# Splitting each head's intra-tile product of a Mamba-2 mixer into two matmuls of 64 result rows

## The reference, cut to what matters

```python
def step(state, inp):
    dA_t, dt_t, B_t, C_t, x_t = inp
    dB = dt_t[:, :, None] * B_t[:, None, :]
    state = dA_t[:, :, None, None] * state + x_t[..., None] * dB[:, :, None, :]
    y = jnp.einsum('bn,bhpn->bhp', C_t, state)
    return (state, y)
...
_, ys = lax.scan(step, state0, xs)
y = ys.transpose(1, 0, 2, 3) + xh * D[None, None, :, None]
y = y.reshape(batch, seqlen, D_SSM)
yg = y * _silu(z)
yn = yg * lax.rsqrt(jnp.mean(yg * yg, axis=-1, keepdims=True) + EPS) * norm_w
return jnp.einsum('bld,ed->ble', yn, W_out)
```

## Time and profile before

| | |
|---|---|
| median of 3 runs | 1515.18 us |
| span of the profiled execution | 1514.6 us |
| PE busy | 1454.3 us (96%) |
| weight loads busy | 1258.6 us (83%) |
| DVE, ACT, POOL busy | 1049.3, 784.3, 788.9 us |
| mean granted TensorE clock | 0.981 |
| line L2184 on PE | 512 passes, 62.6 us busy |

### The profile page before, as it was taken

How to read it: one execution, slowest core, us unless ns; L and a number is a source line. 1 busy time by engine, 2 the same in 40 slices (tenths; PEclk the granted TensorE clock), 3 DMA queues, 4 the chain that set the end, 5 groups by cost and what they waited for, 6 DMA issues and landing times. The chain is left out here.

```text
span 1514.6 us, 22382 instructions
## 1 busy us (share of the span) xinstructions
PE 1454.3 (96%) x8274; PEld 1258.6 (83%) x8274; DVE 1049.3 (69%) x1750; ACT 784.3 (52%) x1343; POOL 788.9 (52%) x480
## 2 busy tenths in 40 slices
PE   6999999999999999999999999999999999999997
PEld 5878999989987687788788779779779999999875
DVE  6584666567556898789769869867746566676455
ACT  3312666666532467566656656645025666666311
POOL 3203777777535445645643753652026777776343
PEclk9899999999999999999999999999999999999998
DMA  8232787787544220020011011016226788876254
GB/s 311 84 115 86 262 279 263 259 278 269 207 155 125 79 88 1 29 70 29 9 62 56 1 43 56 20 32 231 67 82 217 260 280 287 275 259 243 91 161 145
DMA packets 79739, 222.15 MB, mean 147 GB/s; under 512 B 8400, under 2 KB 16592, under 8 KB 78224
## 3 DMA queue, kind: packets, MB, share of 16 engines
q1 hardware_dynamic: 57552, 163.04, 30.9%
q0 software_dynamic: 11360, 37.23, 8.3%
q10 hardware_dynamic: 10720, 20.45, 3.8%
HBM read 183.47 MB, written 37.22 MB: 146 GB/s over the span
## 5 line engine op out<-in xcount | busy, mean ns | idle before, releaser
L661 POOL TENSOR_TENSOR g_lo<-g_raw,g_hi 128x1408 fp32r<-128x1408 f32 x54 | 180.6, 3344 | 113.8 <-ACT g_hi L826 111.3
L661 POOL TENSOR_TENSOR u_lo<-u_raw,u_hi 128x1408 fp32r<-128x1408 f32 x54 | 174.6, 3233 | 59.2 <-ACT u_hi L826 59.1
L1861 PE MATMUL bank<-u_hi,xgT 128*128 128x352 f32 x624 | 168.5, 333 | 0.0
L1884 PE MATMUL bank<-d_hi,hT 128*128 128x512 f32 (+1 forms) x468 | 159.4, 395 | 5.4 <-DVE hT L1166 5.4
L1861 PE MATMUL bank<-g_hi,xgT 128*128 128x352 f32 x624 | 162.9, 323 | 0.0
L691 POOL DMA_INDIRECT xg<-token_x,row_of x78 | 87.9, 1127 | 138.7 <-DVE row_of L1311 122.4
L876 ACT ACTIVATE gate<-bank 128x512 f32<-128x512 f32 (+1 forms) x48 | 28.7, 598 | 213.4 <-PE bank L1814 212.5
L1829 PE MATMUL bank<-d_hi,hT 128*128 128x512 f32 (+1 forms) x384 | 130.7, 413 | 7.8 <-DVE hT L1166 7.6
L747 POOL TENSOR_TENSOR w_hl<-w_raw,w_hl 128x1024 fp32r<-128x1024 f32 x35 | 88.3, 2524 | 95.3 <-ACT w_hl L826 95.3
L721 POOL DMA_INDIRECT yg<-routed_y,slots x64 | 68.7, 1074 | 111.5 <-DVE X L1353 70.9
L1166 DVE TENSOR_TENSOR d_lo<-d_raw,d_hi 96x512 fp32r<-96x512 f32 (+2 forms) x54 | 121.4, 2249 | 0.0
(11 more groups left out here) (264 smaller groups left out, 3669.2 us busy)
## 6 DMA issues: line engine op xcount, KB each, us to landing
g_raw<-in_w_gate SPq DMA_DIRECT2D x54, 704.0 KB, 5.6
u_raw<-in_w_up SPq DMA_DIRECT2D x54, 704.0 KB, 6.9
d_raw<-in_w_down SPq DMA_DIRECT2D x46, 512.0 KB, 5.2
w_raw<-in_w_in SPq DMA_DIRECT2D x36, 512.0 KB, 3.5
routed_y<-ys ACTq DMA_DIRECT2D x32, 512.0 KB
d_raw<-in_w_down SPq DMA_DIRECT2D x46, 192.0 KB, 6.3
token_x<-xn SPq DMA_DIRECT2D x8, 1024.0 KB, 5.8
X<-in_x SPq DMA_DIRECT2D x4, 1024.0 KB, 10.4
```

The source lines that it names most:

```text
L661: pool.tensor_tensor(half_of(piece, 1, s), raw_at[piece][s % RING][:], half_of(piece, 0, s).bitcast(F), ALU.subtract)\
L1861: ins = pe.matmul(dst[:, 0:FE], xgT[:, n % 2, hx, kc], half_of(piece, hw, NS + j)[:, kc], start=(m == 0), stop=(m == 3 * KD - 1))
L1884: ins = pe.matmul(bank[Y + n % 2][:], hT[0:fw, hh, c, 0:P], half_of(2, hw, NS + j)[0:fw, c], start=(m == 0), stop=(m == 3 * NF - 1))
```

## The change

Each head's matmul becomes two. The first takes the first 64 columns of `L[:, h]` as stationary operand and writes rows 0 to 63 of the result, the second takes the last 64 columns and writes rows 64 to 127. The moving operand is the same 128x64 for both. Row and column of the place in the array follow from the operands: the built program holds these matmuls as tiles of 128 rows by 64 columns of the array, at column 0 and at column 64, in turn. Waits and signals stay where they were: a wait before the first matmul of a group, a signal with the last one of two groups.

```diff
                                 for h in range(g * GH, (g + 1) * GH):
-                                    ins = pe.matmul(bank[6 + h // 8][:, (h % 8) * HD:(h % 8 + 1) * HD], L[:, h],
-                                                    xdt[:, h * HD:(h + 1) * HD], start=True, stop=True)
+                                    for r in range(0, P, P // 2):
+                                        ins = pe.matmul(bank[6 + h // 8][r:r + P // 2, (h % 8) * HD:(h % 8 + 1) * HD],
+                                                        L[:, h, r:r + P // 2], xdt[:, h * HD:(h + 1) * HD],
+                                                        start=True, stop=True)
                                 if g % 2:
                                     ins.then_inc(m_E, 1)
```

## The result

The changed kernel takes 1503.43 us (median of 6 runs, 1502.57 to 1512.47), the kernel before 1516.52 us beside it (6 runs, 1514.74 to 1518.38). The ratio is 0.9919, 95% interval 0.9898 to 0.994. I had said 1507 us.

What follows compares the result with a forecast made beforehand. PE was taken to set the pace, in the mixer tile only just, with the burst paced by weight loads. Gains of 1.9 + 5.1 + 1.1 = 8.1 us gave 1507 us; range 1503 to 1545, the forecast's own 1503 to 1512.

Steps and rivals of the forecast that it cites:

- The burst goes at the pace of its loads, and the halves overlap: PE's burst in each mixer tile: both halves load and stream at once, 1.89 us instead of 3.58, 1.69 less.
- rival of one path: All weight loads share one path: +0 to +0.2 us a burst, about 1516 us, no change; chance 0.26.
- slower rivals: Each switch of half costs time (1561 us), or loads and streams don't overlap (1571 us); together chance 0.27.
- Entering and leaving the column tiles: Changing stationary shape around each of 16 bursts: 0 for 32 entries and exits; other end 0.09 each, 2.9 us.
- Tiles 1 and 2: Eight of 16 mixer tiles: POOL's chain limits the gain to 0.24 us each, 1.9 us in all.
- Tile 3: Last tile of a block, projections after it: all 1.69 us kept in three tiles, 5.1 us; the fourth counted 0.
- Tile 0: First tile of a block: 0 in two first blocks, 0.55 us each in two second blocks, 1.1 us.
- The sum: Whole mixer: 1.9 + 5.1 + 1.1 = 8.1 us gained; of 27 us PE would save, 19 lost to POOL.

Runs made afterwards that it cites:

- e1: The changed kernel with, in each group of four heads, first the four upper halves and then the four lower: 1507.76 us, ratio 0.9947.
- e10: The changed kernel with the upper halves of eight heads and then the lower halves of the same eight: 1508.38 us, ratio 0.995.
- e4: The changed kernel with each head as four matmuls of 32 result rows in four column tiles: 1509.88 us, ratio 0.9947.
- e3: The changed kernel with matmuls split only in the second and third tile of each block (8 of 16 bursts): 1512.62 us, ratio 0.9975.
- e6: The changed kernel with POOL's addition of xD to y (L801) done for one of 16 heads only: 1497.74 us, ratio 0.9871.
- e7: The kernel before the change with POOL's addition of xD to y (L801) done for one of 16 heads only: 1519.22 us, ratio 1.0.
- e2: The changed kernel with matmuls split only in the last tile of each block (4 of 16 bursts): 1512.27 us, ratio 0.996.
- e5: The changed kernel again, unaltered, in six more runs: 1506.16 us, ratio 0.9927.

## Why the prediction was right, step by step

- **The burst goes at the pace of its loads, and the halves overlap.** The overlap is shown. 0.117 us a head was measured from the starts (pairs of passes 0.007 apart, 0.058 from pair to pair), 0.118 predicted. e1 and e10 show that it is the alternation that does it. That loads set the pace holds for 128 columns (0.112 a step, 0.058 for 64). Whether load or stream sets it after the change, no run separates: e4, with half the load again, only went from 0.117 to 0.113. For the rival of one path I wrote that loads never overlap each other in the trace; their records do (197 ns long, 112 apart), and only the part that grows with the columns does not. The slower rivals are refuted for this shape: a change of half costs at most the 0.007 within a pair, and load and stream overlap. The rule of the Trainium skill's page "TensorE: Matmul & The Clock Gate", section "Part 3: Packing small matmuls — row/col tiling", that loads overlap with running matmuls only when the row group differs, does not hold here: by it the burst would have been 7.2 us, and it is 2.0.
- **Entering and leaving the column tiles: a term mis-sized.** I took 0 from the passage to 16 columns in the earlier trace rows. The first pass of the burst begins 0.52 us after the last of L2175, where it was 0.43, so the entry costs 0.09, the other end of my bounds; leaving costs 0.04 (0.154 against 0.112 us from the last pass to the next). The Trainium skill's page "TensorEngine Tiling (Array Packing)", section "Key Properties", says that changing the mode drains the engine. A first pass 0.09 us later agrees with that, though no row shows the draining itself; why the passage to 16 columns was free, no run shows. With it the gain is 1.41 us a burst, from the last pass of L2175 to the work behind the burst, and not 1.69. Of the 0.28 less, 0.09 are the entry, and 0.13 the burst itself (2.02 against 1.89), by its first step, 0.107 instead of 0.058, and the way out. The other 0.06 is that the burst before took 3.52 and not 3.58.
- **Tiles 1 and 2: 0.24 us each.** Measured 0.17 to 0.21 in tile 1 (0.46 and 0.44 once each in the two profiles, right behind a first tile that the clock had made longer) and 0.34 to 0.36 in tile 2, 2.5 in all against 1.9. PE's waits before the transposes came to 0.42 + 0.75 = 1.17 us, about 1.4 foreseen. The mechanism is shown by e3, e6 and e7 together.
- **Tile 3: 1.69 us each.** Measured 1.52, 1.33 and 1.49, sum 4.3 against 5.1. The step fell short by what a burst gives, 1.41 and not 1.69, not by POOL's weights, which came just in time as worked out. e2 gives 4.4 in the same tiles. The fourth tile 3, counted as 0, gave 0: from the last burst to the end it is 509.5 us before and after.
- **Tile 0.** In first blocks 0.10 against 0 (and -1.08 once in e5, by the clock). In second blocks 0.55 was predicted; the profile has +1.0 and -0.25, e5 +1.0 and +0.9. The step misread the rows: the last 8 passes of the earlier trace rows step by 0.24, "twice the usual", because the clock was at half from 706.5 on, and this is also why PE came so late to its transposes that there was something to gain. At full clock there is nothing: the unsplit tile of e3 has PE waiting 0.92 and 0.75 us for POOL and is as long as the split one of e10. So the gain here is that of a slowed PE, 0.7 to 1.0 us when the clock falls near the burst (19.39 to 19.41 us after, 20.12 to 20.41 without the split), and it is lost when it falls at another moment (20.55). The chain itself is as foreseen: DVE's additions begin 5.02 us after the burst's start before (708.89 - 703.87) and after. The rows after:

```profile
695.65 1.93 PE L2185 MATMUL bank<-xdt,L 128*64 128x64 f32 x48 [1.93 <-DVE y L1651]
699.01 1.12 PE L2185 MATMUL bank<-xdt,L 128*64 128x64 f32 x16 [1.44 <-DVE L L1639]
```
```profile
700.67 1.27 DVE L1697 TENSOR_TENSOR y<-y,bank 128x512 f32<-128x512 f32 x2
```

  PE's wait for the fourth group of L grew from 0.38 to 1.44 us, so most of what the burst saves there is lost to DVE already.
- **The sum.** 8.1 us predicted, 7.8 measured in the mixer. That it comes so near is partly luck: tile 3 is 0.8 too high, tiles 1 and 2 are 0.6 too low, and tile 0 depends on when the clock falls. The measured medians differ by 11 to 13, and the 4 to 5 us beyond the mixer's go with a clock that the sum did not hold. The time of 1503.43 fell inside the forecast's own range of 1503 to 1512 by 0.4 us, at its low end, and for a reason that I had not named. So the mechanism in the mixer was right, and where in the range the time came to lie was not foreseen.

## What to carry to other kernels

Where short matmuls (64 moving columns of fp32) step at the pace of their weight loads, splitting the stationary operand over two column tiles and alternating between them runs the loads side by side: 1.74 times the pace here (3.52 against 2.02 us), and no further gain with four tiles. Alternate with every matmul, since passes of the other tile began only three places before their turn. And then follow the chain behind the shortened work: here two thirds of some 22 us (16 x 1.4) did not reach the end, most of it for waits on POOL. A second signal in the middle of one POOL addition, worthless before, gave about 8 us once PE was no longer last. Before comparing stretches of two profiles, look at the granted clock in each part of them.

## What the runs showed that I had not expected

- Passes bound for different column tiles do not begin in program order: with 8 passes of a half in a row (e1), the 17th of the program began as the 14th; three go ahead of their turn at each change of half, with 16 in a row (e10) as well.
- Four quarter tiles take 128 passes in 1.99 us, a pace of (1.99 - 0.22) / 127 = 0.014 each, under the 0.025 us that is the quickest step within one place of the array.
- Changing from 128 to 64 stationary columns costs 0.09 us on the way in and 0.04 on the way out, from 128 to 16 nothing that the rows show.
- Between executions of one kernel the mean granted clock ranges from 0.973 to 0.985 in 60 runs of the kernel before, and 0.001 of it is worth 1.06 us, so this range alone is some 13 us.
- An unsplit tile at full clock is as long as a split one where POOL's chain is last (19.38 and 19.39 us in the first tile of a second block); the gain seen in such tiles came with the clock at half.
